# A transformer-like block on one core: the second attention's output projection turned round, with both parts of y made on GpSimd

## What is computed

```python
    x = x + 0.5 * _L0_ffn_ref(_layernorm(x, axis=-1), ...)       # three 128x128 products, tanh
    x = x + _L0_attn_ref(_layernorm(x, axis=-1), ...)            # linear attention
    x = x + 0.5 * _L0_ffn_ref(_layernorm(x, axis=-1), ...)
    x = x + 0.5 * _L1_ffn_ref(_layernorm(x, axis=-1), ...)       # spectral product
    x = x + _L1_attn_ref(_layernorm(x, axis=-1), ...)            # softmax attention, 16 heads of 64
    x = x + 0.5 * _L1_ffn_ref(_layernorm(x, axis=-1), ...)

    # _L1_attn_ref:
    att = jnp.einsum('bhcq,bhCq->bhcC', q, k) / d_query
    att = jnp.where(causal, att, -jnp.inf)
    p = jax.nn.softmax(att, axis=-1)
    y = jnp.einsum('bhcC,bhCv->bhcv', p, v)
    z = jnp.einsum('dvh,bhcv->bcd', W, y) * (math.sqrt(d_embed / d_value) / num_heads)
```

## Time and profile before

| what | value |
|---|---|
| median of 3 runs | 1247.25 us (1246.82 to 1247.5) |
| the profiled execution: its time, its span | 1245.56 us, 1243.5 us |
| TensorE matmul busy, share of the span | 1179.7 us, 95% |
| VectorE, ScalarE, GpSimd busy | 83%, 80%, 50% |
| TensorE in the chain that ended last | 83% |
| project_out (L1157): records, busy | 1024, 132.1 us |
| mean granted TensorE clock | 0.992 |

### The profile page before, as it was taken

One profiled execution on the slowest core, in us unless ns is written; L12 is line 12 of the kernel. 1 busy time (PEld: TensorE's weight loads), 2 busy tenths in 40 slices (PEclk: granted clock), 3 DMA queues, 4 the chain that ended last, 5 costly groups with the idle time before them and its releaser, 6 DMA issues.

```text
span 1243.5 us, 38272 instructions
## 1 busy us (share of the span) xinstructions
PE 1179.7 (95%) x10772; PEld 1027.9 (83%) x10772; DVE 1034.5 (83%) x4904; ACT 995.3 (80%) x3457; POOL 627.1 (50%) x963
## 2 busy tenths in 40 slices
PE   6699977789999999999999999999999999999996
PEld 5589866678888888888888888888888888888885
DVE  7888879978888888888888888888888888888884
ACT  5776748678888888888888888888888888888883
POOL 6644348644444555445554444555545544444443
PEclk9899989999999999999999999999999999999998
DMA  7000000000000000000000000000000000000000
GB/s 231 0 2 0 1 1 1 1 2 2 3 10 0 8 0 8 0 8 0 8 0 8 0 8 0 8 0 8 0 8 0 8 0 8 0 8 0 9 2 18
DMA packets 15243, 11.93 MB, mean 10 GB/s; under 512 B 788, under 2 KB 13400, under 8 KB 15192
## 3 DMA queue, kind: packets, MB, share of 16 engines
q1 hardware_dynamic: 15040, 11.32, 3.1%
q10 hardware_dynamic: 152, 0.00, 0.0%
HBM read 7.13 MB, written 4.19 MB: 9 GB/s over the span
## 4 chain that ended last, share of the span: by engine, by line
PE 83%; DVE 6%; issue 4%; ACT 4%; POOL 1%; SPq 1%; DMA 0%; ACTq 0%; DVEq 0%; POOLq 0%
PE ps L1148 15%; PE ps L1131 13%; PE ps L1157 10%; PE ps L1117 7%; PE ps L1100 7%; PE ps L1113 6%; PE ps L1102 5%; PE ps L1101 5%; PE ps L1139 2%; PE ps L1137 2%; PE ps L1138 2%; PE ps L984 2%; ACT xn L751 1%; PE ps L1001 1%; PE ps L1171 1%
## 5 line engine op out<-in xcount | busy, mean ns | idle before, releaser
L850 ACT ACTIVATE pr<-ps,neg_max 128x128 f32<-128x128 f32 (+1 forms) x1024 | 424.9, 429 | 111.3 <-DVE neg_max L562 111.3
L359 POOL TENSOR_TENSOR pr<-pr,rinv 128x256 f32<-128x256 f32 x256 | 157.9, 617 | 487.3 <-DVE rinv L570 487.3
L562 DVE CUSTOM_DVE_ANT_0 ps<-ps,mask 128x128 f32<-128x128 f32 (+1 forms) x1024 | 329.6, 390 | 0.6 <-issue 0.3
L361 POOL TENSOR_TENSOR pr<-pr,rinv 128x512 f32<-128x512 f32 x256 | 266.6, 1042 | 0.0
L577 DVE COPY pT<-ps 128x512 f32<-128x512 f32 x256 | 176.3, 689 | 63.5 <-PE ps L1131 62.7
L850 ACT ACTIVATION_READ_ACCUMULATOR pr<-ps,neg_max 128x1 f32 x1024 | 216.2, 211 | 0.0
L1131 PE MATMUL ps<-ident,pr 128*128 128x128 f32 x1536 | 210.4, 273 | 2.5 <-POOL pr L361 1.2
L1131 PEld LDWEIGHTS ps<-ident,pr 128*128 128x128 f32 x1536 | 179.6, 141 | 21.5 <-POOL pr L361 2.6
L1148 PE MATMUL ps<-pT,space 128*64 128x256 f32 (+1 forms) x2048 | 194.9, 332 | 0.8 <-ACT pT L859 0.5
L1148 PEld LDWEIGHTS ps<-pT,space 128*64 128x64 f32 x2048 | 126.8, 136 | 55.5 <-ACT pT L859 0.7
L1100 PE MATMUL ps<-x_hi,wqk_hi 128*128 128x256 f32 x512 | 167.9, 328 | 1.6 <-DVE x_lo L536 1.1
(11 more groups left out here) (171 smaller groups left out, 2640.7 us busy)
## 6 DMA issues: line engine op xcount, KB each, us to landing
out<-x_all SPq DMA_DIRECT2D x16, 256.0 KB, 2.3
x_all<-L_attn_x SPq DMA_DIRECT2D x2, 512.0 KB, 6.1
x_all<-L_attn_x SPq DMA_DIRECT2D x2, 256.0 KB, 3.0
space<-L_attn_Q SPq DMA_DIRECT2D x1, 512.0 KB, 5.1
space<-L_attn_K SPq DMA_DIRECT2D x1, 512.0 KB, 6.2
space<-L_attn_V SPq DMA_DIRECT2D x1, 512.0 KB, 7.1
space<-L_attn_W SPq DMA_DIRECT2D x1, 512.0 KB, 7.8
dft_s<-dft SPq DMA_DIRECT2D x1, 192.0 KB, 2.7
```

The lines of the kernel that those rows point to most:

```text
L359: nc.gpsimd.tensor_tensor(pr[:, buf, :, 0, :], pr[:, buf, :, 0, :], r[:, :, 0:1].to_broadcast([P, 2, P]), ALU.mult)
L361: nc.gpsimd.tensor_tensor(pr[:, buf, :, 1:3, :].rearrange("p h b k -> p h (b k)"), pr[:, buf, :, 1:3, :].rearrange("p h b k -> p h (b k)") ...
L562: last = nc.vector.tensor_tensor_reduce(o, o, mask[:, T - w:T], -1.0, -MASKED, ALU.add, ALU.min, neg_max[:, j, 2 * h + qt:2 * h + qt + 1])
L850: last = nc.scalar.activation(dst, ps[:, BANK_S + 2 * j + h, qt * P:qt * P + w], ACT.Exp, bias=neg_max[:, j, at:at + 1], scale=-1.0, accum ...
```

## The change

The projection is turned round and done in the split form. The weight W, times 1/16, becomes wz_hi (fp32r, ScalarE) and wz_lo (a new VectorE operation w_low, into the space of xl_lo). y_out copies y of two pairs to a raw buffer of two places (y_raw, in the space of phq). GpSimd makes y_hi of it, by a multiplication with a one that is broadcast, and y_lo by a subtraction. For every part it first waits: in turn 0 for the second half of z_norm, in turn 6 for ln_soft_norm, in turns 2 and 4 for VectorE's even qk_low. project_out now takes W as the fixed operand and 256 columns of y as the moving one, 24 products in parts of 9, 9 and 6, and the result has the 128 output features on the partitions. ScalarE's o_out copies it to oT, and two transposes (out_transpose) turn it back into BANK_X, behind probs_transpose of turn 5. spectral_product moves behind them. On VectorE probs_T of the even pair moves ahead of add_z and add_spectral. In SBUF several buffers of the phases now share space with those of the softmax batches.

```diff
-        W_STEPS = ((0, 6), (6, 12), (12, 16))
+        W_PAIRS = ((0, 3), (3, 6), (6, 8))
...
+            def y_high(b, jb, p, calls, first=False):
+
+                pool.wait_ge(y_ready, count(calls))
+                if p == 1 and above_0(b - 1):
+                    pool.wait_ge(o_done, count(b - 1))
+                places = y_places(jb, p)
...
+                for to, at in places:
+                    last = nc.gpsimd.tensor_tensor(y_hi[:, to], y_raw[:, (p + 1) // 2 % 2, at],
+                                                   one[:].to_broadcast([P, at.stop - at.start]), ALU.mult)
+                last.then_inc(yhi_ready, 1)
+
+            def y_low(jb, p, calls):
+
+                pool.wait_ge(yhi_ready, count(calls))
+                for to, at in y_places(jb, p):
+                    last = nc.gpsimd.tensor_tensor(y_lo[:, to], y_raw[:, (p + 1) // 2 % 2, at], y_hi[:, to].bitcast(F32), ALU.subtract)
+                last.then_inc(ylo_ready, 1)
...
+                    if p % 2 == 0 and not (first and p == 0):
+                        if p == 0 and above_0(b - 1):
+                            pool.wait_ge(z_xn_ready, count(BT * (b - 2) + BT))
+                        elif p == PAIRS - 2 and has_batch(b + 2):
+                            pool.wait_ge(xn_ready, count(b + (SOFT + 3)))
+                        elif not (last and p == PAIRS - 2):
+                            pool.wait_ge(qklo_ready, count(b * PAIRS + (p + 3)))
+                        if p > 0:
+                            y_high(b, jb, p - 1, b * (PAIRS // 2) + p // 2, first)
+                            y_low(jb, p - 1, b * (PAIRS // 2) + p // 2)
+                        else:
+                            y_high(b - 1, 1 - jb, PAIRS - 1, b * (PAIRS // 2))
+                            y_low(1 - jb, PAIRS - 1, b * (PAIRS // 2))
...
+            def w_low():
+
+                dve.wait_ge(su_hi, 8)
+                nc.vector.scalar_tensor_tensor(out=wz_lo.rearrange("p h d -> p (h d)"), in0=out_weights, scalar=OUT_SCALE,
+                                               in1=wz_hi[:].rearrange("p h d -> p (h d)").bitcast(F32),
+                                               op0=ALU.mult, op1=ALU.subtract).then_inc(su_lo, 1)
...
+            def o_out(b):
+                act.wait_ge(o_done, count(b + 1))
+                nc.scalar.copy(oT[:], ps[:, BANK_X, 0:T]).then_inc(o_ready, 1)
...
-            def project_out(b, j, steps, only=False):
-                pe.wait_ge(y_ready, count(PAIRS // 2 * (b + 1) + 1))
-                for k in range(*steps):
-                    t, p = k // PAIRS, k % PAIRS
-                    last = mm(ps[:, BANK_X, t * D:(t + 1) * D], yT[:, j, p, t * P:(t + 1) * P], wz[:, p, :],
-                              start=(p == 0), stop=(p == PAIRS - 1), skip_group_check=True)
-                if (only or not above_0(b)) and steps[1] == BT * PAIRS:
+            def project_out(b, j, pairs):
+                calls = PAIRS // 2 * (b + 1)
+                for p in range(*pairs):
+                    if p in (0, 3, 5, 7):
+                        pe.wait_ge(ylo_ready, count(calls + (-2, -1, 0, 1)[(0, 3, 5, 7).index(p)]))
+                    of_pair = slice((j * PAIRS + p) * T, (j * PAIRS + p + 1) * T)
+                    mm(ps[:, BANK_X, 0:T], wz_hi[:, p, :], y_hi[:, of_pair], start=(p == 0), stop=False, skip_group_check=True)
+                    mm(ps[:, BANK_X, 0:T], wz_hi[:, p, :], y_lo[:, of_pair], start=False, stop=False, skip_group_check=True)
+                    last = mm(ps[:, BANK_X, 0:T], wz_lo[:, p, :], y_hi[:, of_pair], start=False, stop=(p == PAIRS - 1), skip_group_check=True)
+                if pairs[1] == PAIRS:
+                    last.then_inc(o_done, 1)
+
+            def out_transpose(b, only=False):
+                pe.wait_ge(o_ready, count(b + 1))
+                for t in range(BT):
+                    last = tr(ps[:, BANK_X, t * D:(t + 1) * D], oT[:, t * P:(t + 1) * P], ident[:])
+                if only or not above_0(b):
                     last.then_inc(w_done, 1)
```

More of the change, by code:

```diff
@@ L294, in _ @@
             nc.gpsimd.memset(minus_1[:], -1.0)
+            nc.gpsimd.memset(one[:], 1.0)
             nc.gpsimd.memset(vones[:], 1.0)
@@ L374, in _ @@
             inv_std(SOFT + 1, 1, BT)
+            def y_high(b, jb, p, calls, first=False):
[3 more added lines that the diff above has]
+                places = y_places(jb, p)
+                if first and p == 1:
+                    places = places[1:]
+                    nc.gpsimd.tensor_tensor(y_hi[:, (2 * PAIRS - 1) * T:], y_raw[:, 1, 0:T], one[:].to_broadcast([P, T]), ALU.mult)
+                for to, at in places:
[7 more added lines that the diff above has]
+                last.then_inc(ylo_ready, 1)
             def batch(b, jb, first=False, last=False):
@@ L675, in batch @@
                         qk_low(n + 3, 1)
+                    probs_T(n, 0)
                     if p + 1 == W_TURN + 2 and not first:
@@ L679, in batch @@
                             add_spectral(b - 2, b)
-                    probs_T(n, 0)
                     inv_sum(n + 1, 1)
@@ L867, in values_out, with y_out @@
                 nc.scalar.copy(vv[:, j, c % 2, 512 * (c // 2):512 * (c // 2) + 512], ps[:, bank, :]).then_inc(v_ready, 1)
-            def y_out(b, jb, p, first=False):
+            def y_out(b, p, calls):
                 act.wait_ge(pv_done, count(b * PAIRS + p))
-                if p == 1 and above_0(b - 1):
-                    act.wait_ge(w_done, count(b - 1))
-                at = jb * PAIRS + p - 1
-                if at > 0:
-                    nc.scalar.copy(y_ring[:, (at - 1) * T:(at + 1) * T], ps[:, BANK_Y, :]).then_inc(y_ready, 1)
-                else:
-                    if not first:
-                        nc.scalar.copy(yT[:, 1, PAIRS - 1, :], ps[:, BANK_Y, 0:T])
-                    nc.scalar.copy(yT[:, 0, 0, :], ps[:, BANK_Y, T:2 * T]).then_inc(y_ready, 1)
+                if above_0(calls - 2):
+                    act.wait_ge(ylo_ready, count(calls - 2))
+                nc.scalar.copy(y_raw[:, (p + 1) // 2 % 2, :], ps[:, BANK_Y, :]).then_inc(y_ready, 1)
             def last_y_out():
                 act.wait_ge(pv_done, B * PAIRS)
-                nc.scalar.copy(yT[:, 1, PAIRS - 1, :], ps[:, BANK_Y, 0:T]).then_inc(y_ready, 1)
+                act.wait_ge(ylo_ready, B * (PAIRS // 2) - 1)
+                nc.scalar.copy(y_raw[:, 1, 0:T], ps[:, BANK_Y, 0:T]).then_inc(y_ready, 1)
+            def o_out(b):
+                act.wait_ge(o_done, count(b + 1))
+                nc.scalar.copy(oT[:], ps[:, BANK_X, 0:T]).then_inc(o_ready, 1)
             x_high(0, 0, FIRST_X_BANK)
@@ L912, in batch @@
                         qk_high_odd(n + 3)
+                    if p + 1 == W_TURN + 2 and not first:
+                        o_out(b - 1)
                     exp_head(n + 1, 1, 1, pr_of(p + 1))
@@ L923, in _ @@
             batches(act, batch)
-            y_out(B - 1, 1, PAIRS - 1)
+            y_out(B - 1, PAIRS - 1, B * (PAIRS // 2))
             probs_T(B * PAIRS - 1, 1)
             last_y_out()
+            o_out(B - 1)
         @block.tensor
@@ L1213, in batch @@
                             pe.wait_ge(z_xT_ready, count(b - 1))
-                    if W_TURN <= p < W_TURN + len(W_STEPS) and not first:
-                        project_out(b - 1, 1 - jb, W_STEPS[p - W_TURN])
-                    if p == W_TURN + len(W_STEPS) - 1 and above_0(b - 1):
-                        spectral_product(b - 2)
+                    if W_TURN <= p < W_TURN + len(W_PAIRS) and not first:
+                        project_out(b - 1, 1 - jb, W_PAIRS[p - W_TURN])
                     if p == V_TURN and not last:
@@ L1230, in batch @@
                         probs_transpose(n - 1, 1 - j, pr_of(p - 1), b * (PAIRS // 2) + p // 2)
+                    if p == W_TURN + len(W_PAIRS) - 1 and not first:
+                        out_transpose(b - 1)
+                        if above_0(b - 1):
+                            spectral_product(b - 2)
                     if p % 2 == 1:
@@ L1249, in _ @@
             pe.wait_ge(out_ready, B - 1)
-            project_out(B - 1, 1, (0, BT * PAIRS), only=True)
+            project_out(B - 1, 1, (0, PAIRS))
+            out_transpose(B - 1, only=True)
             spectral_transpose(B - 1)
```

52 lines of the change are left out of this document (34 added, 18 removed).

## The result

| | median | range of the runs | profiled execution: time, span, mean granted clock |
|---|---|---|---|
| before | 1247.03 us | 1245.24 to 1247.5 | 1245.56, 1243.5, 0.992 |
| after | 1237.39 us | 1236.56 to 1238.66 | 1237.79, 1236.1, 0.989 |

The ratio is 0.9926, with an interval of 0.9911 to 0.9941: **0.74% faster**. The first rival, that the turning back costs no wait, gave 1238.4.

The account below looks back on a forecast made before the run. The prediction took TensorE, busy 199.9 of 200 us in the softmax batches, as the bound. From 1245.56 it summed -7.4 (batches), +1.2 (w_low) and +4.5 (tail) to 1243.9, or 1245.6 us on the median's scale, range 1240 to 1252.

Parts of the forecast that it names:

- The first rival: End of the projection: turning back costs no wait, 0.47 instead of 0.24 us gained a batch, 1238.4 us; chance 20%.
- projection, a batch: TensorE's projection: 24 fp32r products replace 16 full fp32 ones, 3.67 to 2.98 us, a gain of 0.69 a batch.
- turning back, a batch: Behind the projection: two added transposes 0.22 us, a wait for ScalarE's oT 0.13 and a pipeline refill 0.10.
- net, times 31: Projection gain less turning back, 0.24 us a batch; 7.4 us less over 31 batches (3.7 to 14.6).
- w_low: One-time VectorE operation ahead of the second FFN's steady turns: 1.2 us more, 0 if the pipeline swallows it.
- POOL: GpSimd's new y parts, 50 to 82% busy: cost nothing, with 0.35 us to spare in turn 0, 0.4 in turn 6.
- tail: Last batch's end: GpSimd's y parts and late add_fft_bias delay the last projection, 4.5 us more (3.5 to 5.5).
- the clock in the tail: Last projection: idle stretches drop TensorE's clock to 0.50, products up to 2.9 us dearer, 1247.6 us; chance 13%.
- the wait of the turning back: Before oT's transposes: TensorE arrives at 1.29, oT allows 1.42 us, so a 0.13 wait and a 0.10 refill.
- half of it: End of the projection: half of the saving from a turning back without wait, giving 1242 us.
- the third rival: Last projection: TensorE's clock falls after idle stretches, up to 2.9 us more for 24 products, 1247.6 us; chance 13%.
- The second rival: Turns 0 and 6: GpSimd's odd-pair scaling comes late and TensorE waits, 1250 to 1259 us; chance 22%.

Follow-up runs that it names:

- the two orders of the tail: After, with GpSimd's last scaling and add_fft_bias(B - 2) ahead of turn 6's part: 1232.82 us; also the last 256 y columns on ScalarE and VectorE: 1232.11 us.
- the short addition on GpSimd: After, with one more GpSimd multiplication of 2 columns (0.20 us) behind every part of y: 1237.64 us.
- The kernel with everything together: After, with the tail reordered on GpSimd, its last 256 y columns made by ScalarE and VectorE, and w_low one turn earlier: 1231.3 us.
- the run with the long addition: After, with one more GpSimd multiplication of 256 columns (0.61 us) behind every part of y: 1245.75 us.

## Why the prediction was wrong

By its own steps, on the span of the profiled executions (it said 1.7 less, the traces say 7.4):

| step | predicted | found |
|---|---|---|
| projection, a batch | -0.69 | -0.74 |
| turning back, a batch | +0.22 + 0.13 + 0.10 | +0.27 to 0.29 |
| net, times 31 | -7.4 | -14.9 (0.481 x 31), of which the traces show 14.4 |
| w_low | +1.2 | about 0.2, within the scatter |
| POOL | 0, margins 0.35 and 0.4 | 0, margins 0.35 to 0.45 |
| tail | +4.5 at full clock | +4.2 |
| the clock in the tail | a rival: up to +2.9 | +2.2 in this execution |

The found values come to 8.3 less and the traces say 7.4. Of the difference 0.5 is the first of the 31 batches: from the first transposes of x in the softmax batches to the first z transposes it is 73.93 us before and 73.90 after, so no saving shows there. The other 0.4 lies ahead of w_low, where the last add of the linear stage starts at 176.78 before and 177.16 after (176.13 in the kernel with w_low earlier), which is scatter.

**The step that failed** is the wait of the turning back: "TensorE comes to them at 6 x 0.12 + 0.57 for the probability transposes (834.45 to 835.02) = 1.29" and "A wait of 0.13 and a refill of 0.10". The 0.57 is the length of those transposes ahead of an fp32r product. Ahead of the fp32 transposes of oT they take 0.66, so TensorE comes at 0.70 + 0.66 = 1.36. The other side was sized from a copy that started 0.39 behind its last product; o_out starts 0.33 behind, takes 0.40, and the transposes can start at 0.58 + 0.33 + 0.40 + 0.05 = 1.36. The wait is the difference of two sums of over a microsecond, each wrong by 0.06 to 0.07 in the direction that shrinks it. The refill was taken from another place, the projection behind z_xT; the run with oT late shows that here there is none even behind a wait of 0.30. That is 0.18 a batch, 5.6 us of the total.
The rival was named with this price and given 20%, and "half of it" as well. The argument against it, that a wait of that size had cost a refill elsewhere, was an argument for the refill only and said nothing on whether there was a wait. That the rival's 1238.4 lies so near the measured 1237.39 is partly luck: its saving in the batches came true, but it also had w_low 1.0 too dear, left out the 2.2 of the clock, and stood on a reference of before that was high.

**The projection** gained 0.05 more than 0.69: 0.118 a product instead of the rounded 0.12, and the two parts that don't wait are at 1.07 and 0.71. That is about 1.5 us over the batches, a rounding multiplied by 24 and by 31. Period, projection and turning back close: -0.74 + 0.27 = -0.47 of -0.48. The later add_z and add_spectral, put at nothing, cost nothing that shows: the scores' stretches are 5.41 us a batch before and 5.43 after.

**w_low** was sized right (1.21) and placed right. That VectorE shows no idle time behind it was taken as proof that it is on the path. It isn't one: VectorE has work to do there, but TensorE's stream over the next 72 us moved by 0.2. The traces can't tell much less than a microsecond in what lies ahead of the batches: kernels that are the same up to there, or whose edits cost nothing (after, the two orders of the tail, the short addition on GpSimd, no waits on the even low part), reached the first z transposes between 322.4 and 324.3 us.

**The tail** is in two parts. From the last batch's first z transposes, the projection starts 27.67 us on where it was 24.25 before; with the 0.48 that the last batch saves, 3.9 later, and 4.1 was predicted. From there to the last z transposes it takes 9.40 instead of 6.83, 2.57 more. The kernel with everything together, whose projection runs at full clock and without a wait, takes 7.16 for this: so 0.3 is the new work, where the prediction had 0.4, and 2.2 the clock, the third rival's. That the clock would fall was right as a mechanism, "TensorE has idle stretches of 2 and 3 us before the last projection", and should have been in the forecast, since its own sum had the idle stretch in front of the projection and the clock had fallen in the tail of before as well.

**POOL** came as predicted in every number: 1.04, 1.28, 82%, and the margins, which the run with the long addition confirms. The second rival (1250 to 1259) would have needed the additional 0.2 to 0.25 on each operation of a part. It was also priced too high: 0.5 on a part was to cost 14 us, and the kernel with 0.61 on a part came to 1245.75, 8.4 above after, because a part of the wait comes back.

**The last two microseconds** lie in which execution stands for which kernel. The profiled executions differ by 7.8 us in time, the medians by 9.6; the median of before was lower, 1245.6 to 1246.2, beside the experiments. The 1.7 that was added to bring the sum to the median's scale was only the scatter of before.

## What to carry to other kernels

What a small group costs on TensorE depends on the kind of the next one, so take the length of a group from a place where the same kind of product follows it; and when the answer is a small difference of two chains, give both signs near-equal chances rather than a wait. A busy stretch without idle time on an engine off the critical path doesn't put an insertion there on the path: count the slack up to the next hand-over. When work moves to GpSimd, look at which VectorE operations it will run beside before looking at GpSimd's load: here four waits a batch turn a loss of 70 us into a gain of 9, and the two on the normalising do all of it. And look at the tail apart: 6.5 of the 14.9 us that the turns gained were lost in it, and another order alone got 3.9 to 4.8 of that back.

## What was not expected of the hardware

- Six fp32 transposes take 0.57, 0.66 or 0.75 us from start to start, by what follows: an fp32r product, an fp32 operation on 128 rows, one on 64 rows. The spectral product takes 0.45 or 0.54 likewise. Why was not tested.
- A wait of TensorE for ScalarE's oT costs its length alone (0.30 for 0.30), one for GpSimd's probabilities 0.06 more, one for z_xT 0.07 to 0.10 more. Why they differ wasn't tested.
- VectorE's normalising of x (0.34 us a half) takes 1.29 in the mean beside GpSimd's parts, each half held to 0.08 us behind the end of the operation that it meets, while that operation stays at 1.04 or 1.28. The odd low part, with one input in PSUM, is not held: 0.55 us beside the same operations.
- After 3.10 us without work TensorE ran 24 products at 0.21 us each, at a granted clock of 0.50; with the same idle stretch in the kernel without the waits on the even low part only the first 15, and in the kernels without that idle stretch they run at 0.118 to 0.12.
